# Adding the residual of an output tile on TensorE instead of VectorE, in three batches of a pipelined scan and FFN kernel

## The reference

```python
# 1. a selective-state-space branch, added to x
xc = silu(causal_conv(in_proj_w @ ctx) + conv_b)            # u
delta = softplus(dt_proj_w @ dt_lo + dt_b)                  # dt_lo, Bm, Cm from x_proj_w @ u
state = state * exp(delta * A) + (delta * u) * B            # a scan over 1024 positions, 16 states
y = (sum_n state * C + D * u) * silu(layernorm(x))
x1 = x + y
# 2. a feed-forward branch with 2 of 8 experts chosen per batch, added to x1
xn = layernorm(x1)
out = xn + sum_over_2_experts(gate * (w2 @ gelu(w1 @ xn + b1) + b2))
result = x1 + (out @ w3.T + b3)
```

## Time and profile before

| | |
|---|---|
| median of 3 executions | 2562.46 us (2556.12, 2562.46, 2563.99) |
| the profiled execution's own time | 2556.93 us |
| its span, first to last instruction | 2555.1 us, mean granted TensorE clock 0.90 |
| busy share of the span | DVE 84%, PE 80%, ACT 60%, POOL 57%, PEld 47% |
| chain that ended last | PE 29%, DVE 18%, issue 15%, ACT 8%, POOL 5% |
| batch 1 to 3 begin at (first scan) | about 604, 1193 and 1789 us; the tail at about 2332 us |

### The profile page before, as it was taken

The page is one execution under the profiler, slowest core; times in us unless marked ns, Lnnn a source line. Parts: engine busy times, 40 slices in busy tenths (PEclk is TensorE's granted clock), DMA queues, the critical chain, the costliest instruction groups (busy, mean ns, idle before and its releaser), DMA issues.

```text
span 2555.1 us, 32784 instructions
## 1 busy us (share of the span) xinstructions
PE 2032.3 (80%) x10840; PEld 1210.5 (47%) x10840; DVE 2157.7 (84%) x2788; ACT 1543.7 (60%) x2237; POOL 1444.5 (57%) x990
## 2 busy tenths in 40 slices
PE   6787778886757897897776888898675797896799
PEld 2666566664433454454443455354443354443244
DVE  5789788878999899999999899998999999995210
ACT  2666466655659658755666657855576858852400
POOL 0577566666756555665775556665775666663000
PEclk9799999997778998998777899999787999998799
DMA  5312323546532544556542364466460274566411
GB/s 169 121 45 72 103 76 118 170 142 214 213 117 83 192 157 143 177 187 195 194 170 90 114 216 142 152 208 199 158 239 25 74 233 148 176 228 218 190 58 66
DMA packets 200186, 382.76 MB, mean 150 GB/s; under 512 B 31537, under 2 KB 97073, under 8 KB 200018
## 3 DMA queue, kind: packets, MB, share of 16 engines
q1 hardware_dynamic: 196848, 380.21, 44.7%
q10 hardware_dynamic: 3170, 0.47, 0.1%
HBM read 346.53 MB, written 34.08 MB: 149 GB/s over the span
## 4 chain that ended last, share of the span: by engine, by line
PE 29%; DVE 18%; issue 15%; ACT 8%; POOL 5%; DMA 1%; SPq 0%; DVEq 0%; POOLq 0%; ACTq 0%
PE dense L1078 11%; DVE h L1450 8%; PE dense L905 6%; POOL h L812 4%; PE dense L843 4%; DVE dense L1426 3%; ACT dA L1195 2%; DVE u L1288 2%; PE dense L855 1%; ACT L1156 1%; PE dense L1008 1%; PE dense L998 1%; PE dense L1055 1%; ACT hs L1262 1%; PE dense L864 1%
## 5 line engine op out<-in xcount | busy, mean ns | idle before, releaser
L812 POOL TENSOR_TENSOR h<-h,Cb 128x1024 f32<-128x1024 f32 x512 | 1208.2, 2360 | 456.0 <-DVE h L1450 432.4
L1195 ACT ACTIVATE dA<-delta,Av 128x512 f32<-128x512 f32 x1024 | 700.6, 717 | 473.5 <-DVE h L1450 471.3
L905 PE MATMUL dense<-ident,h 128*128 128x128 f32 x4096 | 603.2, 298 | 179.4 <-POOL h L812 178.1
L1450 DVE TENSOR_TENSOR_SCAN h<-dA,state,dense 128x512 f32<-128x512 f32 x512 | 628.0, 1265 | 80.0 <-PE dense L905 44.7
L905 PEld LDWEIGHTS dense<-ident,h 128*128 128x128 f32 x4096 | 519.0, 155 | 329.9 <-POOL h L812 244.2
L1450 DVE TENSOR_TENSOR_SCAN h<-dA,dense 128x512 f32<-128x512 f32 x512 | 597.3, 1204 | 46.7 <-PE dense L905 28.6
L1426 DVE TENSOR_TENSOR dense<-dense,Bb 128x512 f32<-128x512 f32 x864 | 551.2, 684 | 1.6
L1078 PE MATMUL dense<-w3h,xT 128*128 128x512 f32 x832 | 390.7, 603 | 0.0
L806 POOL COPY state<-h 128x2 f32<-128x2 f32 x256 | 47.6, 186 | 369.3 <-DVE h L1450 367.8
L891 PE MATMUL dense<-Bb,duT 128*128 128x128 f32 x1280 | 186.0, 292 | 77.3 <-DVE h L1450 72.7
L891 PEld LDWEIGHTS dense<-Bb,duT 128*128 128x128 f32 x1280 | 164.1, 201 | 111.6 <-issue 109.5
(11 more groups left out here) (151 smaller groups left out, 2036.4 us busy)
## 6 DMA issues: line engine op xcount, KB each, us to landing
sww<-in_sw SPq DMA_DIRECT2D x170, 512.0 KB, 4.2
Cb<-bc_scratch SPq DMA_DIRECT2D x64, 512.0 KB, 5.7
Bb<-bc_scratch SPq DMA_DIRECT2D x54, 512.0 KB, 4.4
w3h<-in_sw SPq DMA_DIRECT2D x54, 512.0 KB, 7.7
w3h<-in_w3T SPq DMA_DIRECT2D x52, 512.0 KB, 5.0
row<-x_scratch SPq DMA_DIRECT2D x42, 512.0 KB, 4.5
xz<-in_x SPq DMA_DIRECT2D x64, 256.0 KB, 4.6
xt<-in_x SPq DMA_DIRECT2D x64, 256.0 KB, 4.1
```

The costliest lines, as they stand in the source:

```text
L812: e.tensor_tensor(h[:, s:s + 2, :], h[:, s:s + 2, :], Cb[:, 2 * q:2 * q + 2, :], ALU.mult).then_inc(prod_done, 1)
L905: mm = e.matmul(yT[:, k, :], h[:, 2 * (q % RH) + i, k * P:(k + 1) * P], ident[:], is_transpose=True, start=False, stop=(q == PAIRS - 1 and ...
L1195: e.activation(dA[:, i % RA, :], delta[:, st % 2, :], ACT.Exp, scale=Av[:, j * N + n:j * N + n + 1]).then_inc(dA_done, 1)
L1450: e.tensor_tensor_scan(h[:, 2 * (q % RH) + n % 2, :], dA[:, (N * g + n) % RA, :], dense[:, product_bank(g, n), :], state[:, j * N + n:j * ...
```

## The change

For b < NB (the slots of batches 1 to 3, 48 of the 64 output tiles) TensorE adds the residual: behind the last part of a tile it waits for `res_loaded` and multiplies the 128x128 identity by `res` into the same accumulation, and only then counts up `part_done`. ScalarE then copies the PSUM bank into `res`, and VectorE does nothing for these tiles. In the tail (16 tiles) all stays as it was.

```diff
@@ TensorE, "tile"
                             mm = e.matmul(dense[:, bank, :], xT_of(b, uu)[:, d, k * P:(k + 1) * P], w3[:, d, :],
-                                          start=False, stop=(d == J - 1), skip_group_check=True)
+                                          start=False, stop=(b == NB and d == J - 1), skip_group_check=True)
+                        if b < NB and part == W3C - 1:
+                            n = part_index(b, uu, dh, k, 0) // W3C
+                            e.wait_ge(res_loaded[n % 2], 1 + 16 * (n // 2 + 1))
+                            mm = e.matmul(dense[:, bank, :], ident[:], res[:, n % 2], start=False, stop=True,
+                                          skip_group_check=True)
                         mm.then_inc(part_done, 1)
@@ ScalarE
+                    elif what == "tile_out" and b < NB:
+                        uu, dh, k = a
+                        bank = bank_of(b, "tile", uu, dh, k)
+                        n = part_index(b, uu, dh, k, 0) // W3C
+                        e.wait_ge(part_done, 1 + part_index(b, uu, dh, k, W3C - 1) + 1)
+                        e.copy(res[:, n % 2], dense[:, bank, :]).then_inc(evac[bank], 1)
@@ VectorE
-                    elif what == "tile_out":
+                    elif what == "tile_out" and b == NB:
```

## The result

The changed kernel took 2571.6 us in the median (2566.05 to 2579.44, 12 executions), the kernel before 2557.37 (2552.76 to 2563.99, 12 executions). The ratio is 1.0058, with a 95% interval of 1.0042 to 1.0075: slower by some 15 us (11 to 19). The forecast was +13.7 us.

A forecast was written before the change was run, and what follows sets the result against it. VectorE looked busiest overall, but TensorE was fuller in the first groups of batches 1 and 2. Terms 20.9 - 10.8 - 3.4 + 2 = +8.7, plus 5, gave +13.7 us: median 2576 us, 8 in 10 between 2560 and 2592.

The forecast's parts named there:

- TensorE's product: Identity product per tile in 48 tiles, 0.86 us each: 41.3 us of TensorE, 20.9 us on the path by chain shares.
- VectorE's relief: 48 adds leave VectorE, 28.3 us in all; 10.8 us of them lay on the chain and are saved.
- the waits at the batch ends: Ends of batches 1 and 2: VectorE no longer waits for the last tile's last part; 3.4 us credited.
- What lies beside the chain: 20.4 us of new TensorE work off the chain, where gaps are few; a quarter taken as path, 5 us.
- ScalarE, 2 us: Before its copies ScalarE waits for TensorE, delaying `dA` for VectorE's scans; 2 us taken, bounds nothing to 34 us.
- The room at the tightest tile: Fourth tile of batch 1: ScalarE's next `dA` held up 4.2 us, with 2.2 us remaining before the scan.
- The wait for `res`: TensorE before the identity product, tightest at the fifth tile: value 0, bound 3 x 4 us.
- Where it sits: First groups of batches 1 and 2 longer by about 6 to 8 us each; batch 3's second shorter by 3 to 5.
- its own last sign: Prediction wrong if everything outside the six tile stretches moves by more than a few us.
- Rival 1: All six groups: TensorE's new work is hidden and time falls by 14.2 us to 2548 us; chance 0.08.
- rule of weight loads: First-group stretch without idle TensorE: loads busy 60%, so 40% headroom and the new product hidden.
- Rival 2: Both sides cancel: half of the chain's share is real, +3 us, 2566 us; chance 0.22.

The follow-up runs named there:

- pe_only: TensorE adds the residual in 48 tiles, VectorE instead of ScalarE copies the bank out; against the kernel before, ratio 1.0097 (1.0061 to 1.0132), +25 us.
- act_only: ScalarE copies the 48 tiles, TensorE's identity product left out, so no residual there; against the kernel before, ratio 0.9938 (0.9921 to 0.9955), -16 us.
- as_changed: The changed kernel once more, on the same chip as its two halves; against the kernel before, ratio 1.0053 (1.0034 to 1.0072), +14 us.
- twice: The changed kernel with the identity product made twice in 48 tiles; against the kernel before, ratio 1.0201 (1.018 to 1.0222), +51 us.
- gpsimd_adds: ScalarE copies the 48 tiles into `hs`, GpSimd adds the residual, TensorE gets nothing; against the kernel before, ratio 0.9994 (0.9973 to 1.0014), -2 us.

## Why the prediction was right, point by point

- **TensorE's product, 0.86 us, 20.9 us of 41.3 on the path.** The duration is exact. In `pe_only` 24.1 us were on the path in the stretches and 25 in the timed runs (16 to 34), against 20.9 and, with the 5 us for what lies beside the chain, 26. The total is right by luck in part, because the shares by group were wrong in both directions. The first groups were given 5.9, 5.7 and 3.7 us and grew by 3.4, 4.5 and 1.6; the second groups were given 2.7, 2.8 and 0.2 and grew by 7.0, 5.8 and 1.8. In the second group of batch 2, at the same clock of 0.95, 5.8 of 6.9 us were path where the chain's share had said 41%.
- **VectorE's relief, 10.8 us, and the waits at the batch ends, 3.4 us.** Together 14.2 us against 16 timed in `act_only`. In the stretches it is 19.8 us. The second groups gave 12.3 where the sum had 10.9. The first groups gave 3.5, 0.4 and 3.6 us, where the chain's share had said 0.6, 0.6 and 2.1: 0.4 at an unchanged clock of 0.96, and 3.5 where the clock was 0.97 and the group is 1.1 us shorter even without a change. So a line's share of the chain was neither an upper nor a lower bound of what removing it gave.
- **What lies beside the chain, 5 us, and ScalarE, 2 us.** With both, the sum for the product alone was 26 us and that for the relief 14.2, and 2 us were left for ScalarE. Measured were 25, 16 and a remainder of 5 us between the halves and the whole, which no run assigns. The prediction expected no growth of VectorE's waits for `dA`; they grew by 11.5 us, in `pe_only` by 4.2. The room at the tightest tile, reckoned as in the prediction, was 3.2 us (925.14 less the copy's end at 921.25, less 0.71) and not 2.2, since VectorE's scans came late too.
- **The wait for `res`, 0.** No wait for a DMA stands before line 1083.
- **Where it sits.** Here the prediction was off. It had put 6 to 8 us on each of the first groups of batches 1 and 2 and 3 to 5 us of gain on the last; measured were 2.9 to 4.3 us and 2.2 to 3.4. Its own sum (5.9 less 0.6) gave 5.3. The mis-sized term is TensorE's product and not the relief, for in `pe_only`, without any relief, these groups grew by no more than 3.4 and 4.5 us. The sum had no term for the clock: by the estimate above the product's 6.9 us are all there at full clock, and 3 to 4 us came back because the granted clock was 0.99 instead of 0.96. The second groups of batches 1 and 2, for which the sum had a gain of 0.3 and 0.4 us, lost 0.6 to 2.0.
- **Outside the six groups.** By its own last sign the prediction would be wrong if everything outside them moved by more than a few us. In the first profile it moved by 11 us, but 7.8 of these stand ahead of the first tile. In `as_changed` it moved by 6.3 us, of which 5.3 are the tail, a term that the sum did not have.
- **Rival 1 and the rule of weight loads.** Rival 1 is refuted by `pe_only` and `twice`, and so is the headroom that was read from the weight loads: TensorE had no idle time where they were busy 60%, and at 53% a further product cost its full time. The Trainium skill's page "Perfetto Trace Analysis", section "Identifying the Most-Contended Engine", judges headroom by that share and by MFU, the matmul work done against the peak; MFU was not worked out here. Read as the share of time that is free, the load share misleads for these products of 32-bit floats, since each record holds a load of 0.19 us and lasts 0.43 us.
- **Rival 2, both sides cancel.** Nearly true for the second groups of batches 1 and 2 (+0.6 to +2.0 us); not for the last group, where the relief outweighs the product by 2.2 to 3.4 us, and not for the whole.

## What to carry to other kernels

A share of busy time over the whole program (here VectorE 84, TensorE 80%) does not say which engine an edit should relieve; read both engines' busy time in the stretches that the edit touches, and which one has no idle time there. When work moves from one nearly full engine to another, sum what each side has on the chain, add something for what lies beside it, and check the sum by group, since a right total can hide wrong parts. Here the first product cost 25 us alone, the relief gave 16, and the second product cost 38 to 42 of its 41. Read the granted clock of a stretch beside its length: in the first groups it gave back about half of what the added work cost. When a stretch ahead of the edit differs between two profiles, take it out of the comparison.

## What the runs showed of the hardware

In the changed kernel the same expert stretch took 76.4 us at a mean granted TensorE clock of 0.89 in one execution and 82.1 at 0.81 in another: between the two levels, 1.2 and 2.4 GHz, the clock was at the lower one for a larger part of it. TensorE works in short pieces there and stands idle for a quarter of the time or more (55.05 of 76.4 us busy, 60.09 of 82.7), waiting for VectorE, ScalarE and GpSimd. I had counted on the clock only as a risk on other work. In these profiles it is the largest source of spread that was found. Whether less work on TensorE makes the lower clock likelier stays open: mean granted clocks were 0.887 to 0.899 in `act_only`, 0.894 to 0.904 in the kernel before on the same chip, and 0.901 to 0.910 in `as_changed` and `twice`, which points that way, but `pe_only` with 0.894 to 0.909 does not fit it. By stretch it is no plainer. The first group of batch 2 had 0.99 in all four profiles with one product per tile there and 0.96 in the six in which TensorE and GpSimd do there what they did before. But it had 0.96 with two products (`twice`), and 0.99 in both profiles of `gpsimd_adds`, which has none.
